# Low parts of four GpSimd tiles moved behind the third norm, and the last two loads of x1 and the first output given other places

## What is computed

```python
residual = x                                        # x1 here
h = relu(_bn_train(_conv(x, w1, 1, 0), g1, b1))     # 256 -> 64
h = relu(_bn_train(_conv(h, w2, 1, 1), g2, b2))     # 64 -> 64, 3x3
h = _bn_train(_conv(h, w3, 1, 0), g3, b3)           # 64 -> 256
return relu(h + residual)
```

## Time and profile before

| | |
|---|---|
| median of 3 runs | 870.12 us (868.49 to 870.55) |
| profiled execution, its own time | 867.11 us |
| span of the profiled execution | 865.3 us |
| PE busy | 810.0 us, 94% |
| DVE busy | 649.7 us, 75% |
| ACT busy | 376.1 us, 43% |
| POOL busy | 346.7 us, 40% |
| mean granted clock of TensorE | 0.985 |

### The profile page before, as it was taken

The page is one execution under the profiler, slowest core; times in us unless marked ns, Lnnn a source line. Parts: engine busy times, 40 slices in busy tenths (PEclk is TensorE's granted clock), DMA queues, the critical chain, the costliest instruction groups (busy, mean ns, idle before and its releaser), DMA issues.

```text
span 865.3 us, 13972 instructions
## 1 busy us (share of the span) xinstructions
PE 810.0 (94%) x5084; PEld 767.7 (89%) x5084; DVE 649.7 (75%) x884; ACT 376.1 (43%) x647; POOL 346.7 (40%) x256
## 2 busy tenths in 40 slices
PE   4997988999999999999999999999987979996796
PEld 4997988999999999999999999999977867775685
DVE  4895888898699589768968977896585667129796
ACT  1332112334343434435344444534265697116397
POOL 3317586385267248527723852772200010006200
PEclk9999999999999999999999999999998999999999
DMA  9920515987895996779499688747389896020498
GB/s 264 375 103 1 98 28 134 216 215 179 178 244 127 230 180 190 201 166 244 126 234 177 180 212 165 205 116 209 67 249 297 229 322 266 0 81 17 181 424 367
DMA packets 249932, 162.18 MB, mean 187 GB/s; under 512 B 191833, under 2 KB 232778, under 8 KB 247178
## 3 DMA queue, kind: packets, MB, share of 16 engines
q1 hardware_dynamic: 241162, 144.52, 63.1%
q10 hardware_dynamic: 8704, 16.78, 6.3%
HBM read 99.48 MB, written 56.36 MB: 180 GB/s over the span
## 4 chain that ended last, share of the span: by engine, by line
PE 76%; DVE 8%; POOL 5%; issue 4%; DMA 4%; ACT 1%; SPq 1%; DVEq 0%; POOLq 0%; ACTq 0%
PE ps L1088 21%; PE ps L1090 21%; PE ps L1089 21%; PE ps L1158 4%; PE ps L1174 3%; PE ps L1206 3%; POOL xbuf L777 2%; PE ps L1113 1%; POOL ring L766 1%; DMA w1raw<-in_L_conv_w 1%; DVE y L1850 1%; DMA xq<-in_x 1%; POOL whole L761 1%; DVE hT L1436 1%; DVE whole L1524 1%
## 5 line engine op out<-in xcount | busy, mean ns | idle before, releaser
L766 POOL TENSOR_TENSOR ring<-whole,ring 128x576 fp32r<-128x576 f32 x112 | 188.5, 1687 | 272.3 <-ACT ring L847 272.3
L1088 PE MATMUL ps<-w_hi,ring 128*128 128x336 f32 x832 | 277.7, 334 | 9.6 <-DVE me L1601 7.4
L1090 PE MATMUL ps<-w_hi,ring 128*128 128x336 f32 x832 | 265.0, 319 | 0.0
L1089 PE MATMUL ps<-w_lo,ring 128*128 128x336 f32 x832 | 264.0, 317 | 0.0
L1088 PEld LDWEIGHTS ps<-w_hi,ring 128*128 128x128 f32 x832 | 159.7, 192 | 10.4 <-issue 7.9
L1089 PEld LDWEIGHTS ps<-w_lo,ring 128*128 128x128 f32 x832 | 159.6, 192 | 0.0
L1090 PEld LDWEIGHTS ps<-w_hi,ring 128*128 128x128 f32 x832 | 158.6, 191 | 0.0
L847 ACT ACTIVATE ring<-whole 128x576 fp32r<-128x576 f32 x112 | 87.2, 779 | 107.6 <-POOL whole L761 55.5
L847 ACT ACTIVATE band_hi<-ps 128x320 fp32r<-128x320 f32 (+1 forms) x128 | 53.0, 418 | 132.7 <-PE ps L1158 125.6
L1524 DVE SCALAR_TENSOR_TENSOR whole<-xbuf 128x576 f32<-128x576 f32 x80 | 88.4, 1107 | 14.5 <-POOL ring L766 7.5
L1088 PE MATMUL ps<-band_hi,xT_hi 128*128 128x224 f32 (+2 forms) x320 | 95.2, 298 | 1.4 <-DVE xT_lo L1436 1.1
(11 more groups left out here) (165 smaller groups left out, 1366.6 us busy)
## 6 DMA issues: line engine op xcount, KB each, us to landing
xq<-in_x SPq DMA_DIRECT2D x116, 256.0 KB, 4.7
raw<-bands SPq DMA_DIRECT2D x32, 768.0 KB, 6.9
xbuf<-in_x SPq DMA_DIRECT2D x16, 1024.0 KB, 8.7
x_dram<-x ACTq DMA_DIRECT2D x32, 512.0 KB, 5.7
x1in<-x_dram SPq DMA_DIRECT2D x7, 2048.0 KB, 13.2
bands<-wide SPq DMA_DIRECT2D x64, 199.0 KB, 4.7
out<-x1in SPq DMA_DIRECT2D x12, 1024.0 KB, 6.2
w1raw<-in_L_conv_w SPq DMA_DIRECT2D x2, 3136.0 KB, 12.7
```

Source lines behind the costliest of these rows:

```text
L766: pool.tensor_tensor(split(k, 1), positions(whole[:, k % TBUFS, :], 0, 2), split(k, 0).bitcast(F32), ALU.subtract).then_inc(sig_lo_done, 1)
L1088: pe.matmul(dst, l_hi, r_hi_, start=first, stop=False, **kw)
L1089: pe.matmul(dst, l_hi, r_lo_, start=False, stop=False, **kw)
L1090: return pe.matmul(dst, l_lo, r_hi_, start=False, stop=last, **kw)
```

## The change

GpSimd computes the low parts of tiles 4 to 7 only after `BN3_END`. Load 6 goes into `y[:, 0:4]` and waits for the first four tiles alone. Load 7 goes into `y[:, 4:8]`, waits for all eight turned tiles and low parts, and stands on SP behind the two stores of output 0. Output 0 is made in place 0 of `x1in`, where load 7 went before, and ACT waits there for the sums of the third norm.

```diff
         def x1_place(u):
 
-            return y[:, 4:8, :] if u == 6 else x1in[:, (2, 3, 4, 5, 6, 1, None, 0)[u], :, :]
+            return y[:, 4 * (u - 6):4 * (u - 6) + 4, :] if u >= 6 else x1in[:, (2, 3, 4, 5, 6, 1)[u], :, :]
 
         def out_place(u):
 
-            place = x1_place(u - 1) if u else y[:, 0:4, :]
+            place = x1_place(u - 1) if u else x1in[:, 0, :, :]
...
             load_x1(5)
-            sp.wait_ge(hT_ps, 16)
-            sp.wait_ge(h2_lo_done, 8)
+            sp.wait_ge(hT_ps, 8)
+            sp.wait_ge(h2_lo_done, 4)
             load_x1(6)
-            sp.wait_ge(sums_ps, 1)
-            sp.wait_ge(bn_dve, BN3_READ)
-            load_x1(7)
             for u in range(8):
+                if u == 1:
+                    sp.wait_ge(hT_ps, 16)
+                    sp.wait_ge(h2_lo_done, 8)
+                    load_x1(7)
                 store_out(sp, u)
...
                 pool.wait_ge(centered, 2 * i + 2)
+                if i == 4:
+                    pool.wait_ge(bn_dve, BN3_END)
                 pool.tensor_tensor(h2_lo[:, i, :], y[:, i, :], h2_hi[:, i, :].bitcast(F32), ALU.subtract
...
                 if u == 0:
-                    act.wait_ge(hT_ps, 16)
-                    act.wait_ge(h2_lo_done, 8)
+                    act.wait_ge(sums_ps, 1)
```

## The result

The changed kernel takes 871.67 us (median of 16 runs), the kernel before 868.43 us (16 runs beside them). The ratio, estimated from all of these runs, is **1.0043**, 95% interval 1.0032 to 1.0053, or 3.7 us slower (2.8 to 4.6); the two medians lie 3.2 us apart. The profiled execution has a span of 868.5 us.

What follows compares the result with a forecast made beforehand. DVE was taken to bound the covariance stage, computing and backlogged transfers together the last. Computing would end 2.9 us earlier, but load 7, landing 7.9 us later, sets the end: 870.1 + 2.9 = 873.0 us, range 870.0 to 875.5.

Steps and rivals of the forecast that it cites:

- The saving: Covariance stage: without GpSimd's stalls of DVE's centring in tiles 5 to 7, it ends 2.88 us earlier.
- GpSimd beside the last stage: Last stage: forecast charged no stall; a rival had GpSimd and L1886 hold each other, 877.9 us, chance 0.04.
- the stalls stay: Rival, covariance stage: the centring L1850 is long for another reason than POOL; +5.8, 875.9 us, chance 0.03.
- The issue of load 7: Last stage: SP issues load 7 at 824.4, after POOL's last low part, 8.4 us later than before.
- The landing of load 7: Last stage: load 7 takes 8.9 us from issue and lands at 833.3, against 825.4.
- The follower: Last stage: the first of the 14 stores behind load 7, forecast to land 2.46 us after it.
- The stores' pace: Last stage: the 14 stores behind load 7 land 2.46 us apart, the last at 867.8, against 864.9.
- 825.4 + 16 x 2.46: Kernel before, last stage: load 7's landing plus 16 store times gives 864.8, where the last store landed.
- the sum: Whole kernel: the last landing comes 2.9 us later, so 870.1 + 2.9 = 873.0 us.
- The rival of the cheap load in a queue: Last stage: a load with stores right behind costs them only two store times; +0.3, 870.4 us, chance 0.20.
- The rival that transfers do not bind: Last stage: the saving is whole and the last store lands at 862.0; 867.2 us, chance 0.05.

Runs made afterwards that it cites:

- e3: Changed kernel without load 7 (last block's residual left out, DVE waiting for seven loads only); ratio 0.9969 to the kernel before.
- e5: Changed kernel with GpSimd's low parts of tiles 4 to 7 waiting for the covariance stage's last cast, load 7 ahead of all stores; ratio 0.9969.
- e4: Changed kernel with the stores of outputs 1 to 7 held on SP until load 7 has landed; ratio 1.0063 to the kernel before.
- e8: Changed kernel with a store of 2048 KB in the place of load 7; ratio 1.0018 to the kernel before.
- e9: Changed kernel with only half of load 7 (two tiles of four, 1024 KB); ratio 1.0015 to the kernel before.
- e1: Changed kernel without GpSimd's wait for BN3_END, load 7 still behind the two stores of output 0; ratio 1.0055 to the kernel before.
- e2: As e1, with load 7 ahead of all stores as well; ratio 1.0008 to the kernel before.
- e10: Changed kernel with load 7 issued by ACT before its eighth activation of the last stage, not by SP; ratio 1.0033 to the kernel before.
- e6: As e5, but tile 7's low part waits for BN3_END and load 7 is cut into three tiles and one; 864.59 us, ratio 0.9965.

## Why the prediction came out as it did

- **The saving**, 2.88 forecast, was 2.87, and e3 shows that it reaches the end if no transfer is in its way. The stalls of tiles 5 to 7 went, DVE's wait for ACT in tile 6 was 0.53 us, and ACT's copy of block 15 began at 805.23, which is 806.52 on the scale of the trace before, with 806.54 forecast.
- **GpSimd beside the last stage**: 2.39 us a tile, no stall of L1888, no wait of PE. Shown by e3. That rival and the one that the stalls stay are out. L1888 reads one tensor in SBUF and isn't held (1.28 us); L1877 in e5 reads two and is (0.45 us, against 0.16 for the same step in the kernel before).
- **The issue of load 7**, 824.4 forecast, was 823.19, which is 824.48 on the scale of the trace before.
- **The landing of load 7** is the term that was mis-sized: 8.9 us forecast, **10.5** measured. I took it from loads with nothing, or only late stores, behind them; e4 gives 8.8 for that case. The follower, forecast at 8.9 + 2.46 = 11.4 us after the load's issue, came at 13.0. With nothing behind the load it is no better: e4's follower came 8.8 + 3.9 = 12.7 us after the issue. So the step that failed is that stores follow 2.46 us behind a load that took as long as one alone. e8 shows that the direction matters, and e9 that the size does, by more than the bytes; why stays open.
- **The stores' pace**, 2.46 forecast, was 2.45 up to the last one. That the transfers bind with load 7 in its late place, on which all hung, is shown by e1, e2 and e3 together. In the kernel before they did not bind at the end: that 825.4 + 16 x 2.46 meets its last landing does not show that they set it, for e2 ends at the same time with load 7 landed 7.6 us earlier.
- With 10.5 for 8.9 the sum is +4.5 and not +2.9; the trace gives +4.4 from a common start. The timed difference, 3.7 (2.8 to 4.6), takes in both +4.4 and the forecast +2.9, the latter at its edge. The median of 871.67 came out below 873.0 although the change cost more than forecast, because the kernel before ran at 868.43 beside it, and not at 870.12. That the two errors go opposite ways and leave only 1.3 us is luck; on 870.12 the time would have been 873.8.
- The rival of the cheap load in a queue is out: with a queue behind it the load took 1.7 us more than alone, and the follower needed 13.0 us from the load's issue, where this rival makes it 1.44 + 4.92 + 2.46 = 8.8. The rival that transfers do not bind is out by the last store's 11.2 us.

## What to carry to other kernels

When a last stage ends with stores, look at landings and not at the mean busy share. Landings at one constant distance mean a backlog, and the last store tells whether it reaches the end: 3.9 us from issue to landing where it did not (the kernel before, e2, e3), 11.2 where it did. Then whatever is put into the queue lands on the end, even from another engine's queue (e10). Before delaying an engine to spare another, list the transfers that wait for it; here 2.9 us of computing were won and 7.3 us of landing lost through one load of 2 MB. Nearly all of the saving (2.8 us in e6) was to be had without the loss, by putting GpSimd's work under a chain of small steps that reads mostly PSUM, which kept the load early.

## What the hardware showed beside that

With a load from DRAM at the head of a queue of stores the engines moved 286 GB/s at a busy share of 1.01 (828 to 832 in the changed kernel), where stores in its place moved 429. A load with nothing behind it reached 391 GB/s at a share of 1.00 (830 to 832 in e4). Why the two directions get in each other's way stays open.

Code loading (the packets of the queue named instruction) rides on the same 16 DMA engines. In e3 it has one packet in the stretch from 824 to 825 (6.0% of 16 engines for 1 us, which is about one engine for that time); behind it stand the landings of the stores issued at 820.40 and 822.78:

```profile
q8 instruction: 1, 0.02, 6.0%
...
out<-x1in SPq DMA_DIRECT2D x1, 1024.0 KB, 4.4
...
out<-x1in SPq DMA_DIRECT2D x1, 1024.0 KB, 5.8
```

They land at 824.8 and 828.6, 3.8 us apart and not 2.46, and all behind keep the delay until there is slack. Such packets come twice in the last stage of each trace, 19 to 30 us apart. Within a backlog the gap between landings behind one is often longer than 2.45 us: by 1.3 us in e1 (849.9 to 853.6), 1.7 in e4 and 0.8 in e8. But it need not be. The second packet of the changed kernel falls into its backlog at 846.8, and the landings around it, of the stores issued at 834.47 and 837.27, stay 2.4 us apart:

```profile
q8 instruction: 1, 0.02, 5.8%
...
out<-x1in SPq DMA_DIRECT2D x1, 1024.0 KB, 14.0
...
out<-x1in SPq DMA_DIRECT2D x1, 1024.0 KB, 13.6
```

Both packets of the kernel before (828.1 and 847.9) leave its landings 2.4 to 2.5 us apart as well. That a packet delays one engine, and with it each landing, is inferred from the times, and what decides whether it does stays open. For the experiments it means that nets from one trace may differ by 1 to 2 us for this reason alone (an estimate from these gaps).
